# Normalising x features first instead of turning it on TensorE, and running the scores and maxima over all 128 rows

## The reference, cut to what matters

```python
x: (8, 1024, 512)                       # batches, tokens, features; 16 heads of 32
x = x + attn(layernorm(x))
x = x + ffn(layernorm(x))               # token-mixing ffn
# attn: ct_q = xn @ Wd_q + b;  query = ct_q @ Wu_q + b + rope(ct_q @ Wq_r + b)
#       ct_kv = xn @ Wd_kv + b; key = ct_kv @ Wu_k + b + rope(xn @ Wk_r + b); value = ct_kv @ Wu_v + b
#       softmax(query @ key.T / scale) @ value, per head;  then @ Wo + bo
```

## Time and profile before

| | |
|---|---|
| median of 3 runs | 2982.26 us |
| profiled execution: its own time | 2981.69 us |
| its span, first to last instruction | 2979.9 us |
| mean granted clock of TensorE in it | 0.996 |
| PE busy in the span | 2944.0 us (99%), 15360 matmuls |
| DVE / POOL / ACT busy | 2175.6 / 2021.9 / 1481.6 us |
| fold, projection (chunks 0 to 14) | 0 to 49.9, 49.9 to 593.4 us |
| projection, chunk 15 with the maxima | 593.4 to 646.4 us |
| attention | 653.2 to 2239.1 us |
| mix | 2239.1 to 2979.9 us |

### The profile page before, as it was taken

The page is one execution under the profiler, slowest core; times in us unless marked ns, Lnnn a source line. Parts: engine busy times, 40 slices in busy tenths (PEclk is TensorE's granted clock), DMA queues, the critical chain, the costliest instruction groups (busy, mean ns, idle before and its releaser), DMA issues. The chain is left out here.

```text
span 2979.9 us, 42725 instructions
## 1 busy us (share of the span) xinstructions
PE 2944.0 (99%) x15360; PEld 2002.6 (67%) x15360; DVE 2175.6 (73%) x3372; ACT 1481.6 (50%) x2716; POOL 2021.9 (68%) x704
## 2 busy tenths in 40 slices
PE   8999999989999999999999999999998999999999
PEld 5888888865555555555555555555547888888887
DVE  5555555587777777777777777777787766776774
ACT  2222222226666666666666666666673333333232
POOL 1111111119999999999999999999954666566664
PEclk9999999999999999999999999999999999999999
DMA  4545555664656555555555555555542323323221
GB/s 153 170 172 179 174 172 172 207 166 109 133 124 132 125 130 126 130 127 128 128 128 129 126 131 125 131 124 133 133 125 90 112 58 113 97 72 113 88 81 43
DMA packets 195226, 380.74 MB, mean 128 GB/s; under 512 B 24544, under 2 KB 59520, under 8 KB 187136
## 3 DMA queue, kind: packets, MB, share of 16 engines
q1 hardware_dynamic: 186144, 313.71, 38.3%
q0 software_dynamic: 8928, 65.02, 10.7%
HBM read 194.59 MB, written 118.49 MB: 105 GB/s over the span
## 5 line engine op out<-in xcount | busy, mean ns | idle before, releaser
L430 DVE TENSOR_REDUCE part_max<-ps_m 128x1 f32<-128x512 f32 x1984 | 1209.8, 682 | 303.6 <-PE ps_m L421 303.6
L1145 POOL TENSOR_TENSOR pairs<-probs 128x2048 f32<-128x2048 f32 x248 | 1155.1, 4667 | 101.7 <-ACT probs L1119 101.7
L1119 ACT ACTIVATE probs<-ps_s 128x512 f32<-128x512 f32 x2012 | 1014.5, 625 | 261.9 <-PE ps_s L1010 245.8
L421 PE MATMUL ps_m<-k_stack,q_stack 96*128 96x512 f32 x1984 | 813.2, 410 | 6.7 <-PEq L469 6.7
L1010 PE MATMUL ps_s<-q_stack,k_stack 97*128 97x512 f32 x2012 | 795.6, 397 | 0.0
L421 PEld LDWEIGHTS ps_m<-k_stack,q_stack 96*128 96x128 f32 x1984 | 377.2, 190 | 272.1 <-DVE part_max L430 155.1
L1023 PE MATMUL ps_o<-probs,v_tiles 128*32 128x512 f32 x4096 | 492.5, 598 | 0.0
L1010 PEld LDWEIGHTS ps_s<-q_stack,k_stack 97*128 97x128 f32 x2012 | 380.1, 189 | 122.3 <-ACT probs L1119 2.8
L683 POOL TENSOR_TENSOR ln_rstd<-ln_rstd,ln_minus_half 128x4 f32<-128x4 f32 x15 | 15.1, 1009 | 403.9 <-DVE ln_rstd L725 403.9
L1152 POOL TENSOR_TENSOR pairs<-pairs 128x2048 f32<-128x2048 f32 x62 | 284.1, 4582 | 4.9
L1023 PEld LDWEIGHTS ps_o<-probs,v_tiles 128*32 128x32 f32 x4096 | 106.9, 109 | 229.1 <-issue 172.1
(11 more groups left out here) (196 smaller groups left out, 4767.2 us busy)
## 6 DMA issues: line engine op xcount, KB each, us to landing
pairs<-pairs POOLq DMA_DIRECT2D x62, 1024.0 KB, 7.8
q_stack<-q_hi_scratch SPq DMA_DIRECT2D x128, 256.0 KB, 5.4
k_stack<-k_hi_scratch SPq DMA_DIRECT2D x64, 512.0 KB, 10.4
x_in<-in_x SPq DMA_DIRECT2D x16, 1024.0 KB, 5.7
q_hi_scratch<-st_hi SPq DMA_DIRECT2D x64, 256.0 KB, 2.3
q_lo_scratch<-st_lo SPq DMA_DIRECT2D x64, 256.0 KB, 2.5
k_hi_scratch<-st_hi SPq DMA_DIRECT2D x64, 256.0 KB, 2.4
k_lo_scratch<-st_lo SPq DMA_DIRECT2D x64, 256.0 KB, 2.6
```

Of the source, the lines that this page charges most:

```text
L421: nc.tensor.matmul(bank[:, :], att["q"][r][0:ROWS, half, h, q * P:(q + 1) * P], att["k"][r][0:ROWS, h, kc * CH:(kc + 1) * CH], start=True, ...
L430: nc.vector.reduce_max(part_max[:, half, j, kc:kc + 1], banks[u % MR][:, :], AX).then_inc(att["m_read"], 1)
L1119: nc.scalar.activation(probs[:, (r * UNITS + u) % PR, x // HG, x % HG, :], bank(n, place(u * UT + x))[:, :], ACT.Exp, scale=SCALE).then_in ...
L1145: nc.gpsimd.tensor_tensor(pairs[:, w, :, :], probs[:, (r * UNITS + u) % PR, 0, :, :], probs[:, (r * UNITS + u) % PR, 1, :, :], ALU.add).th ...
```

## The change

Two parts, made together.

*Projection.* x is fetched a second time with the features in the partitions, from an input `xT` that holds it turned. DVE no longer normalises x; it turns the 8 statistics of a token tile (mean and the power -1/2) with a 32x32 transpose, SP stores them to DRAM in four DMAs and loads them back as two rows broadcast to all partitions, and POOL normalises the turned x with 8 operations of 128x512. ACT's `x_hi` and DVE's `x_lo` read SBUF now. The turns leave PE.

*Attention.* Scores and maxima read all 128 rows of both stacks. Rows 96 to 127 are set by engines: -1 in `k_stack`, 0 in `q_stack` (DVE for slot 0 in the fold, POOL for slot 1 in chunk 15 and for slot 2 at the start of the attention). Row 96 of `q_stack` holds old maxima when a slot is loaded again, so each such load has one more small DMA of zeros. The stack of the second half of the maxima of group 0 moves from the end of the projection's SP program to the start of the attention's.

```diff
 # fold
+            sp.dma_start(ahead["xt"][1][:], xT_v[0, 1]).then_inc(ahead["xt_loaded"][1], 16)
...
-            nc.vector.memset(att["k"][0][ROWS:ROWS + 1, :, :].bitcast(F32), -1.0)
+            nc.vector.memset(mv[:, TPC:, :], 0.0)
+            rows_behind_the_stacks(nc.vector, att, 0)
 # helpers
+def loaded_count(loads):
+    return 16 * (LOADS * loads + loads - 1)
+def rows_behind_the_stacks(engine, att, r):
+    engine.memset(att["q"][r][ROWS:P, :, :, :].bitcast(F32), 0.0)
+    return engine.memset(att["k"][r][ROWS:P, :, :].bitcast(F32), -1.0)
 def load_group(sp, att, scratch, n, r):
+    if not (type(n) is int and n == r):
+        zeros = att["q"][0][ROWS + 1:ROWS + 2, 0, 0:1, :].bitcast(F32)
+        sp.dma_start(att["q"][r][ROWS:ROWS + 1, :, :, :].bitcast(F32).rearrange("o c a t -> o (c a) t"),
+                     zeros.broadcast_to([1, NQ * HG, CH])).then_inc(att["loaded"][r], 16)
 # max_product; the stacks' views are [:, ...] now, so the scores read 128 rows too
-    nc.tensor.matmul(bank[:, :], att["q"][r][0:ROWS, half, h, q * P:(q + 1) * P],
-                     att["k"][r][0:ROWS, h, kc * CH:(kc + 1) * CH], ...)
+    nc.tensor.matmul(bank[:, :], att["q"][r][:, half, h, q * P:(q + 1) * P],
+                     att["k"][r][:, h, kc * CH:(kc + 1) * CH], ...)
 # projection
-    TURNS = {3: (0, 1), 5: (2, 3)}
+    LOWS = {8: (0, 1), 9: (2, 3)}
+    STATS_STORED, STATS_LOADED = 0, 2
 # SP: behind the stores of item 0 and of item 2
+            def store_stats(c, par):
+                sp.wait_ge(mv_done, c + 1)
+                by_column = stats_d[par].rearrange("k s p -> s k p")
+                for b in range(BLOCKS):
+                    sp.dma_start(by_column[:, :, b * BLOCK:(b + 1) * BLOCK],
+                                 mv_turned[b * BLOCK:b * BLOCK + 2 * TPC, :]).then_inc(stats_stored, 16)
+            def load_stats(c, par):
+                sp.wait_ge(stats_stored, 16 * BLOCKS * (c + 1))
+                if not is_first(c):
+                    sp.wait_ge(x_normed, c * FC)
+                sp.dma_start(row_stats[:].rearrange("p k t -> p (k t)"),
+                             stats_d[par].rearrange("(o k) s p -> o (k s p)", o=1).broadcast_to([P, 2 * CH])).then_inc(stats_loaded, 16)
...
-                        sp.wait_ge(transposed, c * FC + FC)
+                        sp.wait_ge(xlo_done, c * FC + FC)
                         sp.dma_start(x_in[par][:], x_v[i + 1, par]).then_inc(x_loaded[par], 16)
+                        sp.dma_start(xt[par][:], xT_v[i + 1, par]).then_inc(xt_loaded[par], 16)
...
-            stack_max(sp, held, att, 0, 0, 1)
 # PE: transpose() and its calls are gone
-                            for f in TURNS.get(n, ()):
-                                transpose(c + 1, 1 - par, f)
 # ACT: x_hi copies from xt, all four after the item-7 copies, each behind x_normed
-                nc.scalar.copy(xT_hi[par][:, f, :], ps_t[f % TR][:, :]).then_inc(xhi_done, 1)
+                nc.scalar.copy(xT_hi[par][:, f, :], xt[par][:, f, :]).then_inc(xhi_done, 1)
 # POOL, behind the rope sums of the chunk
+            def normalise(c, par, loads):
+                pool.wait_ge(xt_loaded[par], 16 * loads)
+                pool.wait_ge(stats_loaded, 16 * c)
+                for f in range(FC):
+                    nc.gpsimd.tensor_tensor(xt[par][:, f, :], xt[par][:, f, :], row_stats[:, 0, :], ALU.subtract).then_inc(centred, 1)
+                for f in range(FC):
+                    pool.wait_ge(centred, (c - 1) * FC + f + 1)
+                    nc.gpsimd.tensor_tensor(xt[par][:, f, :], xt[par][:, f, :], row_stats[:, 1, :], ALU.mult).then_inc(x_normed, 1)
...
+                    if last and par == CPB - 1:
+                        pool.wait_ge(xlo_done, B * CPB * FC)
+                        rows_behind_the_stacks(nc.gpsimd, att, 1)
 # DVE: normalise() becomes
+            def turn_stats(c):
+                dve.wait_ge(rstd_done, c + 1)
+                if not (type(c) is int and c == 1):
+                    dve.wait_ge(stats_stored, 16 * BLOCKS * (c - 1))
+                nc.vector.transpose(mv_turned[:, :], mv[:, :, :].rearrange("p s k -> p (s k)")).then_inc(mv_done, 1)
-                nc.vector.tensor_tensor(xT_lo[par][:, f, :], ps_t[f % TR][:, :], xT_hi[par][:, f, :],
+                nc.vector.tensor_tensor(xT_lo[par][:, f, :], xt[par][:, f, :], xT_hi[par][:, f, :],
 # attention
+            stack_max(sp, held, att, 0, 0, 1)
             for s in att["v_stored"]:
                 sp.wait_ge(s, 16 * B * CPB)
-            for r in range(1, R3):
-                sp.dma_start(ks[r][ROWS:ROWS + 1, :, :].bitcast(F32),
-                             ks[0][ROWS:ROWS + 1, :, :].bitcast(F32)).then_inc(rows_set, 16)
-                if u == 0 and x == 0 and type(n) is int and n == 1:
-                    pe.wait_ge(rows_set, 16 * (R3 - 1))
+                if type(n) is int and n == 1:
+                    pe.wait_ge(slot2_filled, 1)
+            rows_behind_the_stacks(nc.gpsimd, att, 2).then_inc(slot2_filled, 1)
+            pool.wait_ge(slot2_filled, 1)
```

More of the change, by code:

```diff
@@ L664, in body @@
                         high(c, n)
-                        if not (last and par == CPB - 1):
-                            for f in TURNS.get(n, ()):
-                                x_hi(c + 1, 1 - par, f)
                     for k in range(2):
@@ L672, in body @@
                         nc.scalar.copy(st_hi[:, n % RING, :], g0[:, k, :]).then_inc(hi_done, 1)
+                    if not (last and par == CPB - 1):
+                        for f in range(FC):
+                            x_hi(c + 1, 1 - par, f)
             body(0, False)
```

87 lines of the change are left out of this document (44 added, 43 removed).

## The result

The changed kernel takes **2962.73 us** (median of 4 runs, 2960.54 to 2965.09), beside 2982.38 (2982.16 to 2984.54) for the kernel before: ratio 0.993, 95% interval 0.9918 to 0.9943. It is faster, by 19.7 us (0.7%); 38.3 were forecast, and the time lies outside the range of 2931 to 2961. The profiled execution took 2960.96 us (span 2959.2, mean granted clock 0.995).

What follows compares the result with a forecast made beforehand. PE was taken to bound projection and attention. Turns -26.3, fold +3.5, projection's end -2.4, rows -12.4 and chunk 15 -0.7 gave -38.3 us: 2981.69 to 2943.4, plus 0.6 for the median, 2944.0 us; range 2931 to 2961.

Steps and rivals of the forecast that it cites:

- The turns: Projection: removing PE's turns of x saves 1.75 us in each of 15 chunks, -26.3 us.
- rival 4: Projection: DVE shuts POOL out, x_lo comes 9.6 us late per chunk, +144 us, 3088 us; chance 0.05.
- rival 3: Projection: the statistics' broadcast is as late as a k_stack load, +22 us, 2966 us; chance 0.08.
- This holds if the new way of getting x_lo ends before PE wants it: Projection: condition for the turns' saving; x_lo done at about 31 us of a 34.5 us chunk, 3.5 us of cover.
- Behind SP's new wait stand the stores of items 3 to 7: Projection: stores queued behind SP's wait for the statistics have over 10 us from their ring of four.
- The fold: Start of the kernel: also filling q_stack on DVE delays PE's third product, +3.5 us, ends 0 and 7.
- The end that the forecast had named but not taken: Fold: the 7 us end, if a PE pause of the fill's length also costs clock.
- The end of the projection: Pause before the attention: four DMAs move behind the engines' meeting, -2.4 us; chunk 15's rows give another -0.7.
- The rows: Attention: scores and maxima over 128 rows start closer together, -12.4 us, ends 0 and -22.
- If over 128 rows they start as 128-row matmuls do elsewhere, 12 of the 15 distances fall to 0.227: Attention: a unit's sixteen matmuls take 3.52 us for 3.61, -0.09 a unit, -22 us in all before any hold.
- The last score waits for the exponential of the fifth: Attention: waiting for its bank limits a unit's gain to a mean of 0.05 us, 248 units, -12.4 us.
- Rival 1: Attention and chunk 15: the rows make no difference, 2957 us; chance 0.25.

Runs made afterwards that it cites:

- fold_and_spread: Changed kernel with the two fills issued by POOL and the first group's ten loads spread over chunk 14's stores: 2949.27 us, ratio 0.9889.
- fold_on_pool: Changed kernel with the two fills of rows 96 to 127 of the first stacks issued by POOL instead of DVE in the fold: 2953.55 us, ratio 0.9899.
- rows_only: Changed kernel with x turned on PE as before, so the attention's part of the change alone: 2979.63 us, ratio 0.9986.
- after: The profile of the changed kernel itself, no further edit: profiled execution 2960.96 us.
- exp_384: Changed kernel with ACT's exponentials reading 384 of 512 columns for every group after the first: a group 0.22 to 0.33 us shorter.
- probe_rows: Changed kernel with some projection matmuls of chunks 2 to 13 reading only rows 0 to 96 of their usual tiles: 2966.03 us.
- probe_stream: Changed kernel with projection matmuls that signal one by one, change banks or wait for satisfied semaphores, as the attention's do: 2960.73 us.
- probe_place: Changed kernel with some projection items taking operands from the stacks, with varied or constant data, or from other weight tiles: 2965.38 us.
- narrow_exp: Changed kernel with ACT's exponentials over 64 of 512 columns for every group after the first: group 49.32 us, middle distances 229.3 ns.
- fold_and_group: Changed kernel with the fills issued by POOL and chunk 14's ten loads of the first group issued behind the statistics' broadcast: 2952.91 us.

## Why the prediction was wrong

- **The turns: right.** Chunks 1 to 13 took 34.45 us, 1.79 less each for the 1.75 forecast. The broadcast, issued at 13.3 of a chunk (14), landed at 17.9 (17); it took 4.6 us for the 2.9 assumed, POOL ended at 28.9 (27.3), the last x_lo at 31.8 (31). Two of POOL's eight operations stood beside DVE's subtractions of two SBUF operands and took 1.74 us each, the others 1.29: rival 4's mechanism is there and costs 0.9 us of cover. Rivals 3 and 4 are out; that rival 3's 2966 lies nearest to the measured time is chance, as the broadcast took 4.4 to 5.1 us from issue to landing in every chunk.
- **"This holds if the new way of getting x_lo ends before PE wants it": wrong in chunk 14.** The sentence "Behind SP's new wait stand the stores of items 3 to 7" looked at what is queued behind the wait and not at what stands in the queue ahead of it. The broadcast waits for stores that stand behind 3.5 MB of loads. The chunk took 5.4 us more, and PE ran at 1.2 GHz behind the wait. `fold_and_spread` removes it with the same loads.
- **The fold: +3.5 was too little.** The third product starts 4.5 us later, its wait 4.1 longer: the fill and a 0.80 gap before DVE's next one. The end that the forecast had named but not taken, that the pause costs clock as well, came: the product behind the wait takes 1.7 us more at 1.2 GHz. In the profiled execution the fold gets as much back, as the later stretch at 1.2 GHz is not in it, and ends 4.4 late; that stretch comes in chunk 0, which takes 1.7 us more than chunk 1. In most other profiles the fold ends 8 to 10 late. `fold_on_pool` is 9.2 us under the changed kernel (medians, 2962.73 to 2953.55), though by the scatter noted above not all of it need be the fills'.
- **The end of the projection: half right.** The pause is 4.12 us for 4.3. Chunk 15 with the pause gave 1.2 for 3.1: its first seven matmuls ran at 1.2 GHz behind chunk 14's wait, 1.5 us, and its distances did not move (232.4 ns for 232.7 on average), since every fourth matmul still changes place. Where nothing delays its start, in `rows_only` and `fold_and_spread`, it gave 2.3 and 2.7.
- **The rows: the step that failed.** "If over 128 rows they start as 128-row matmuls do elsewhere, 12 of the 15 distances fall to 0.227": they fell to 0.232. The difference between 0.227 and 0.234 was read as a price of 96 rows; it is a price of changes. What the change took away is the change of rows, between maxima of 96 and scores of 97 and towards the 128-row products with probs: 25 ns a unit in `after`, 248 x 0.025 = 6.2 us, of which 1.3 are lost again outside the sixteen matmuls (the stage gave 4.9); in `rows_only` it gave 7.4. The other changes of operands stay. "The last score waits for the exponential of the fifth" was right: its load ends the wait for ACT and precedes it by 0.11 in the unit shown. But this is no limit of the last distance alone: with it gone (`exp_384`) distances all along the second half of the unit fall. The mis-sized term is the forecast's -12.4 us: its 0.05 a unit was worked out for the last score only and assumed that the others were at 0.227 by then. The stage measured -4.9. Rival 1 (2957) was nearer than the forecast, though not true either: the rows do make a difference.
- The Trainium skill's statement on loading weights ("TensorE: Matmul & The Clock Gate", section "LDWEIGHTS (loading the stationary operand)"), that the rows don't count, was weighed and set aside for the row that shows 0.234. `probe_rows` agrees with the page: 97 rows run at 226.7 ns once nothing changes.

The sum of the misses: chunk 14 5.4, attention 7.5, the end of the projection 1.9, chunk 0's clock 1.7, fold 0.9, mix 0.8, less 0.6 won more at the turns: 17.6, which is 38.3 - 20.7 of the spans.

Not settled: what in TensorE makes a change of place or rows cost ten or five distances. It was not tried whether the stacks' place matters by itself or by their last 32 rows, which are constant there. Nor is it known why every fourth unit of `exp_384` has the short sequence, or what makes a group of the attention take 49.65 us in some executions and 49.56 in others. The mix takes 740.1 to 741.5 us over the profiles with its code unchanged, so its 0.8 us show nothing.

## What to carry to other kernels

Where two streams of matmuls differ by a few ns, compare where they change, not what they are: here a stream ran at the same pace over 97 rows as over 128, and lost it with the two in turn. A wait for a small DMA must be checked against everything in its queue in every iteration, the last ones with their extra loads above all. A few us on an engine that idles are better than one fill on the chain, since the waits of TensorE in the fold and in chunk 14 were paid a second time in clock.

## What the runs showed of the hardware

- A matmul of 512 columns with alternating weights starts every 226.7 ns at 2.4 GHz, whatever it signals, waits for (if satisfied) or writes to (`probe_stream`).
- A change between 97 and 128 rows costs 26 ns over five distances, a change of the operands' place 50 ns over ten, repeated to the ns in twelve chunks (`probe_rows`, `probe_place`); changes at every second or fourth matmul, or one operand of each matmul in the other place, hold the mean at 233 to 234 ns.
- ScalarE's exponentials of 512 columns, one every 0.48 us beside two matmuls of 0.453, cost TensorE 0.22 to 0.33 us a group; with 384 columns they keep up and cost nothing, and less reading brings nothing further (`exp_384`, `narrow_exp`).
- POOL and DVE fill 4096 elements a partition on 32 partitions in 3.51 and 3.47 us; DVE takes 3.47 on one partition too.
- Stores of 256 KB that take 2 to 3 us to land take 12 to 15 behind 3.5 MB in the same queue (`after`), and 16 to 17 in `fold_and_group`.
